# TensorE takes over more of the neighbour sums of a two-layer attention kernel

## The reference, cut to what matters

```python
# layer 0, per dilation: kp, vp are the nine shifted copies of k and v, zero outside the image
attn = softmax(einsum('bhdn,bhdkn->bhnk', qh, kp) * scale)
out = einsum('bhnk,bhdkn->bnhd', attn, vp)        # a sum of nine products per pixel
x = x + concat(outs[i] * gate[:, i])
# layer 1: 4 heads of 32 channels
p = W_qkv @ gn(x) + b_qkv                         # q = k = v = p
att = softmax(p @ p.T / 16)                       # 32x32 per head
x = x + W_proj @ (att @ p) + b_proj
```

## Time and profile before

| | |
|---|---|
| median of three runs | 83.10 us (83.10 to 83.11) |
| the profiled execution | 83.13 us, span 81.3 us |
| VectorE busy | 67.5 us, 83% |
| TensorE busy (matmul) | 71.1 us, 87% |
| GpSimd busy | 41.5 us, 51% |
| ScalarE busy | 29.3 us, 36% |

### The profile page before, as it was taken

The page is one execution under the profiler, slowest core; times in us unless marked ns, Lnnn a source line. Parts: engine busy times, 40 slices in busy tenths (PEclk is TensorE's granted clock), DMA queues, the critical chain, the costliest instruction groups (busy, mean ns, idle before and its releaser), DMA issues.

```text
span 81.3 us, 2474 instructions
## 1 busy us (share of the span) xinstructions
PE 71.1 (87%) x1010; PEld 51.4 (63%) x1010; DVE 67.5 (83%) x184; ACT 29.3 (36%) x92; POOL 41.5 (51%) x84
## 2 busy tenths in 40 slices
PE   4999998799995698999969797879999999999950
PEld 4999753466742466776857664567676868575530
DVE  2152999999999989999999699889999888597850
ACT  1762765963384000000030003230994271764200
POOL 7104018912930037999999999699990005100000
PEclk9999999999999999999999999999999999999999
DMA  1980055000000000000000000000000000012253
GB/s 27 315 286 18 0 120 142 7 0 8 0 0 4 0 12 0 0 0 4 8 0 0 0 0 0 8 0 0 0 0 8 0 0 12 0 57 72 73 194 129
DMA packets 2796, 3.06 MB, mean 38 GB/s; under 512 B 352, under 2 KB 2400, under 8 KB 2784
## 3 DMA queue, kind: packets, MB, share of 16 engines
q1 hardware_dynamic: 2496, 2.63, 10.5%
q10 hardware_dynamic: 288, 0.26, 0.9%
HBM read 1.84 MB, written 1.05 MB: 36 GB/s over the span
## 4 chain that ended last, share of the span: by engine, by line
DVE 54%; PE 28%; POOL 7%; issue 5%; ACT 2%; POOLq 0%
PE ps L815 27%; DVE qk L602 18%; DVE pv L643 12%; POOL rstd L342 3%; POOL acc L379 3%; DVE acc L655 3%; DVE pv L655 2%; DVE x L674 2%; DVE prob L622 2%; DVE smax L609 2%; DVE ssum L619 2%; POOL pv L379 2%; DVE sums L570 1%; DVE acc L643 1%; PE ps L972 1%
## 5 line engine op out<-in xcount | busy, mean ns | idle before, releaser
L815 PE MATMUL ps<-prob,sel 64*128 64x192 f32 (+6 forms) x192 | 17.8, 313 | 2.7 <-DVE pv L643 1.6
L643 DVE TENSOR_TENSOR pv<-ps,v 128x128 f32<-128x128 f32 (+7 forms) x32 | 17.1, 567 | 1.8 <-PE ps L815 0.8
L815 PEld LDWEIGHTS ps<-prob,sel 64*128 64x128 f32 x192 | 13.7, 186 | 6.9 <-DVE pv L643 3.5
L815 PE MATMUL ps<-xn,wp 128*32 128x256 f32 (+1 forms) x208 | 17.1, 384 | 0.9 <-ACT q L417 0.7
L815 PE MATMUL ps<-idle 128*128 128x128 f32 x82 | 14.6, 328 | 1.1 <-DVE idle L533 1.1
L379 POOL TENSOR_TENSOR pv<-pv 128x240 f32<-128x240 f32 (+3 forms) x24 | 14.1, 600 | 0.5 <-DVE pv L643 0.5
L815 PEld LDWEIGHTS ps<-idle 128*128 128x128 f32 x82 | 12.6, 231 | 2.4 <-DVE idle L533 1.1
L342 POOL TENSOR_TENSOR rstd<-gvar,mhalf 128x2 f32<-128x2 f32 (+1 forms) x6 | 4.9, 809 | 15.9 <-DVE gvar L549 15.9
L379 POOL TENSOR_TENSOR acc<-acc,pv 128x256 f32<-128x256 f32 (+4 forms) x20 | 12.7, 640 | 0.5
L815 PEld LDWEIGHTS ps<-xn,wp 128*32 128x32 f32 (+1 forms) x208 | 8.7, 116 | 6.1 <-ACT xn L443 1.3
L602 DVE TENSOR_TENSOR qk<-q,k 128x672 f32<-128x672 f32 (+7 forms) x21 | 11.4, 607 | 0.0
(11 more groups left out here) (82 smaller groups left out, 89.6 us busy)
## 6 DMA issues: line engine op xcount, KB each, us to landing
out_dram<-x SPq DMA_DIRECT2D x8, 128.0 KB, 1.8
gx<-x_dram SPq DMA_DIRECT2D x2, 256.0 KB, 4.4
gx<-x_dram ACTq DMA_DIRECT2D x2, 128.0 KB, 3.1
sel<-selc_dram SPq DMA_DIRECT2D x4, 64.0 KB, 2.2
wp<-wpack_dram SPq DMA_DIRECT2D x1, 194.0 KB, 4.2
gx<-x_dram SPq DMA_DIRECT2D x1, 192.0 KB, 2.8
wp<-wpack_dram SPq DMA_DIRECT2D x1, 131.0 KB, 2.2
gx<-x_dram SPq DMA_DIRECT2D x1, 128.0 KB, 3.0
```

What stands on the lines that cost most here:

```text
L643: last = nc.vector.tensor_tensor(o, a, b, ALU.mult)
L815: return nc.tensor.matmul(o, w, m, start=start, stop=stop)
```

## The change

- GpSimd sums (0,0) to (0,3) and (1,0) whole as before, and does only the first five adds of (1,1) (`POOL_ADDS`). None of the second half's other sums are its work. Its two roots stand after the eighth add of (1,0) and the third of (1,1).
- `add_neighbours` is gone from VectorE. `add_last` makes six adds after the last multiply: column sums of (1,2) and (1,3).
- `restore` and `sum_second` become `add_tiles`: 32x32 tiles everywhere. The first half is brought back in one go, behind `spread(1,1,1)`. In the second half TensorE adds slots 4, 3, 5, 1, 7 of (1,2), 4, 3, 5, 1, 0, 2, 7 of (1,3) and 4, 1, 7, 8 of (1,1); it does so for batches j = 0, 1 first (group 2) and then for j = 2, 3 (group 3), each in an early and a late list.
- The order on all engines: projections of group 0 stand between the last spreads; the rest of groups 0 and 1 stands behind the sums. All `keep_clock` calls after the first half's last spread are gone. One more `norm` is on VectorE.

```diff
-NORMS_ON_DVE = ((2, 0), (3, 0), (3, 1))
-NORMS_ON_ACT = ((0, 0), (0, 1), (1, 0), (1, 1), (2, 1))
+NORMS_ON_DVE = ((2, 0), (2, 1), (3, 0), (3, 1))
+NORMS_ON_ACT = ((0, 0), (0, 1), (1, 0), (1, 1))
...
-POOL_SUMS = (ND, 2)
-
-RSQRT_AFTER = ((1, 0, 4), (1, 1, 0))
+POOL_ADDS = ((8, 8, 8, 8), (8, 5, 0, 0))
+
+RSQRT_AFTER = ((1, 0, 7), (1, 1, 2))
...
@@ ScalarE's order @@
             for i in range(2):
+                copy_projection(0, i)
+            for i in range(2):
                 norm(1, i)
...
             squares(2)
             squares(3)
+            for i in range(2):
+                copy_pT(0, i)
+            for i in range(2):
+                copy_projection(1, i)
+            copy_projection(2, 0)
+            attention_exp(0)
...
@@ VectorE @@
                 if ph and chunk == 0:
-                    dve.wait_ge(added, ADDS * (s + 1))
+                    dve.wait_ge(added, added_by(0, s))
+                    if s == LAST_UNIT:
+                        dve.wait_ge(restored, SLOTS)
...
-            def add_neighbours(ph, s):
...
-            def add_last_column():
...
+            def add_last():
+
+                steps = ((2, 7, 6, 0), (3, 7, 6, 0), (2, 1, 0, 0), (2, 7, 8, 1), (3, 7, 8, 2), (2, 1, 2, 3))
                 dve.wait_ge(pv_ready, 12 * PHASES)
...
-            multiply_pv(1, 1, 0)
+            for i in range(2):
+                multiply_pv(1, 1, i)
             first_residual(0)
-            multiply_pv(1, 1, 1)
-            second_variance(0)
             first_residual(1)
             multiply_pv(1, 1, 2)
+            second_variance(0)
+            multiply_pv(1, 2, 0)
             second_variance(1)
-            for i in range(2):
-                multiply_pv(1, 2, i)
+            multiply_pv(1, 2, 1)
             second_norm_bias(0)
-            second_norm_bias(1)
             multiply_pv(1, 2, 2)
             multiply_pv(1, 3, 0)
-            add_neighbours(1, 2)
+            second_norm_bias(1)
             for i in range(1, 3):
                 multiply_pv(1, 3, i)
-            add_last_column()
+            add_last()
+            first_residual(2)
+            second_variance(2)
+            first_residual(3)
+            second_norm_bias(2)
+            for i in range(2):
+                norm(2, i)
+            second_variance(3)
             attention_shift(0)
+            second_norm_bias(3)
+            for i in range(2):
+                norm(3, i)
+            attention_divide(0)
...
@@ TensorE @@
+            def add_tiles(ph, tiles, js, stop, finished=False):
+
+                for s, slot in tiles:
+                    if slot == 4:
+                        t, first, (r0, r1), (c0, c1) = acc, (ph * ND + s) * N, (0, H), (0, W)
+                    else:
+                        ci, ri = divmod(slot, 3)
+                        t, first, (r0, r1), (c0, c1) = pv[s], slot * N, valid_rows(s, ri), columns(DIL[s], ci)[:2]
                     dims = [[W, r1 - r0], [1, c1 - c0]]
                     at = r0 * W + c0
-                    for j in range(SLOTS):
+                    for j in js:
                         rows = slice(32 * j, 32 * j + 32)
-                        last = mm(view(ps, 512 * (BANK[2] + j) + at, dims, 32 * s, 32), ident[rows, rows],
-                                  view(t, first + at, dims, 32 * j, 32), start=start, stop=stop)
-                        if stop and s == LAST_UNIT:
+                        last = mm(view(ps, 512 * (BANK[GROUPS // PHASES * ph] + j) + at, dims, 32 * s, 32),
+                                  ident[rows, rows], view(t, first + at, dims, 32 * j, 32),
+                                  start=slot == 4, stop=(s, slot) in stop)
+                        if finished and (s, slot) == tiles[-1]:
                             last.then_inc(restored, 1)
...
-            spread(1, 1, 0)
-            restore(0)
-            spread(1, 1, 1)
+            for i in range(2):
+                spread(1, 1, i)
...
+            pe.wait_ge(added, added_by(0, LAST_UNIT))
+            add_tiles(0, [(s, 4) for s in range(ND)], range(SLOTS), stop=[(s, 4) for s in range(ND)], finished=True)
+            spread(1, 1, 2)
             group_stats(0)
-            restore(1)
-            spread(1, 1, 2)
+            spread(1, 2, 0)
             group_stats(1)
...
-            for i in range(2):
-                project_second(0, i)
+            project_second(0, 0)
+            spread(1, 3, 1)
+            project_second(0, 1)
+            spread(1, 3, 2)
+            ends = ((0, 4), (1, 8), (2, 7), (3, 7))
+            early = [(2, 4), (3, 4), (2, 3), (3, 3), (2, 5), (3, 5), (0, 4), (3, 1), (3, 0), (3, 2)]
+            pe.wait_ge(pv_ready, 12 * PHASES - 1)
+            pe.wait_ge(added, added_by(1, 0))
+            add_tiles(1, early, range(2), stop=ends)
+            pe.wait_ge(last_added, 6)
+            pe.wait_ge(added, added_by(1, 1))
+            add_tiles(1, [(2, 1), (1, 4), (3, 7), (1, 1), (2, 7), (1, 7), (1, 8)], range(2), stop=ends, finished=True)
+            add_tiles(1, early, range(2, SLOTS), stop=ends)
+            group_stats(2)
+            add_tiles(1, [(2, 1), (1, 4), (3, 7), (1, 1), (2, 7), (1, 7), (1, 8)], range(2, SLOTS), stop=ends, finished=True)
+            for i in range(2):
+                transpose(0, i)
             for i in range(2):
                 project_second(1, i)
+            group_stats(3)
+            project_second(2, 0)
+            attention(0)
+            project_second(2, 1)
+            transpose(1, 0)
+            project_second(3, 0)
+            transpose(1, 1)
+            project_second(3, 1)
+            for i in range(2):
+                transpose(2, i)
+            attention(1)
             for i in range(2):
                 fuse(0, i)
...
```

More of the change, by code:

```diff
@@ L219, in build @@
         added = sem("added")
-        dve_added = sem("dve_added")
         last_added = sem("last_added")
@@ L940, in tile @@
                             last.then_inc(restored, 1)
-                pe.wait_ge(pv_ready, 12 * PHASES)
-                pe.wait_ge(added, ADDS * sum(POOL_SUMS))
-                pe.wait_ge(dve_added, ADDS)
-                for s in range(ND):
-                    tile(s, acc, (ND + s) * N, start=True, stop=s != LAST_UNIT)
-                s = LAST_UNIT
-                for slot in (3, 5, 1, 0, 2, 7):
-                    ci, ri = divmod(slot, 3)
-                    if slot == 7:
-                        pe.wait_ge(last_added, 2)
-                    tile(s, pv[s], slot * N, *valid_rows(s, ri), *columns(DIL[s], ci)[:2], stop=slot == 7)
@@ L1067, in _ @@
+            add_tiles(1, early, range(2, SLOTS), stop=ends)
+            group_stats(2)
+            add_tiles(1, [(2, 1), (1, 4), (3, 7), (1, 1), (2, 7), (1, 7), (1, 8)], range(2, SLOTS), stop=ends, finished=True)
+            for i in range(2):
+                transpose(0, i)
             for i in range(2):
                 project_second(1, i)
-            for i in range(2):
-                transpose(0, i)
-            for i in range(1, 3):
-                spread(1, 3, i)
-            transpose(1, 0)
@@ L1081, in _ @@
-            keep_clock(2, BANK[1] + 1)
-            group_stats(2)
-            finish(0, 0)
-            keep_clock(2, BANK[1] + 1)
-            group_stats(3)
-            finish(0, 1)
-            keep_clock(1, BANK[1] + 1)
+            for i in range(2):
+                transpose(3, i)
+            attention(2)
+            for i in range(2):
+                finish(0, i)
             for i in range(2):
                 fuse(1, i)
+            attention(3)
             for i in range(2):
-                project_second(2, i)
@@ L1092, in _ @@
-            transpose(2, 0)
-            project_second(3, 0)
-            transpose(2, 1)
-            project_second(3, 1)
-            attention(2)
-            for i in range(2):
-                transpose(3, i)
-            finish(1, 0)
-            attention(3)
-            finish(1, 1)
+                finish(1, i)
             for i in range(2):
```

99 lines of the change are left out of this document (29 added, 70 removed).

## The result

The changed kernel takes 92.69 us in the median (91.92 to 93.07), the kernel before 83.1; the ratio is 1.116, 95% interval 1.107 to 1.125. The direction was as forecast, the size was not: 92.7 lies far outside 82.9 to 86.0. The profiled execution took 91.92 us with a span of 90.0.

A forecast was written before the change was run, and what follows sets the result against it. VectorE (54% of the chain) and TensorE (28%) were taken as the bound; VectorE's gain is eaten by TensorE's queue, so the last residual moves from 79.06 to 80.8, +1.7 us on 83.13: 84.8 us, range 82.9 to 86.0.

The forecast's parts named there:

- a rival with 0.05: TensorE's clock falls to the lower level, doubling 5 to 8 us of its work, partly hidden: 87 to 89 us; chance 0.05.
- TensorE has gaps then, at most 1.0 us by my schedule (50.9 to 51.9, waiting for squares): With fillers gone, TensorE idles at most 1.0 us, which costs nothing unless the clock falls.
- The last product: VectorE's last product ends at 59.2 us instead of 63.17, one small step of six caught beside GpSimd; span 58.8 to 60.1.
- the second root: VectorE waits some 0.3 us at the second bias for GpSimd's second root, ahead of (1,3)'s later chunks.
- Later than forecast, 86: Rival: all small steps are caught beside GpSimd and the spreads wait longer, 86 us; chance 0.10.
- VectorE free 3.2 us sooner: After the last product, `add_last` takes 1.25 us and ends at 60.5 us, where VectorE's adds had ended at 63.69.
- The sums: Second half on TensorE: each list lasts as long as its fullest column group, early 1.3 us, late 1.6 us, both run twice.
- tiles don't run side by side: Rival: the 32x32 tiles' column groups run in turn, early list 2.8 us, late 2.4, total 87 us; chance 0.04.
- What has moved behind: After `project_second(3,0)` starts at 69.75 us, TensorE has 9.8 us of work and 0.7 of waits; last residual ends at 80.8.
- The faster: Rival: layer 0's last residual sets the end and TensorE's backlog fits into its gaps, 82.5 us; chance 0.13.
- the same rival: Rival: lists take 1.2 us instead of 1.6 and VectorE has no new waits, 83.1 us; chance 0.08.
- the gaps without them cost nothing: After the first half's last spread, TensorE's gaps without fillers, at most 1.0 us, cost nothing unless the clock falls.

The follow-up runs named there:

- the run with short additions: Changed kernel, no fillers, 11 of GpSimd's 13 second-half additions cut to two elements: three executions 84.50 to 84.54 us, one 92.09; ratio 1.019.
- the single round: Changed kernel with fillers in all three gaps, second half's sums made once for all four batches instead of twice for two: 84.53 us, ratio 1.019.
- the reordered kernel: Kernel before with (1,2)'s sums moved to TensorE in one round and the engines' lists in a new order: 82.49 us, ratio 0.995.

## Why the prediction was wrong in size, step by step

**The clock.** The fall was a rival with 0.05. Its condition is met: the stage behind 58.4 us runs at half pace. The step that failed is "TensorE has gaps then, at most 1.0 us by my schedule (50.9 to 51.9, waiting for squares)", and with it the 0.05 for a fall. I had listed the gap of 0.92 and missed 0.34 and 1.23 us, since I took VectorE as never idle and did not ask whether TensorE is, while VectorE is at steps that no spread waits for. In the 17.1 us at half pace TensorE was busy 16.7, work of some 8.3 us at full clock, against the 5 to 8 counted. What was mis-sized is the part that others hide: 87 to 89 us let 2.2 to 4.2 of 5 to 8 us reach the end, and 5.95 of some 8.3 did.

The Trainium skill, page TensorE: Matmul & The Clock Gate, section "Part 1: The HAM clock gate", says that the throttle is the resting state and that activity lifts it. The traces agree as far as gaps precede the fall. They differ in what follows it: TensorE was busy for 4.00 of 4.00 us from 68 to 72 and the granted clock stayed at 0.50; by the page alone one would have counted on an early return.

**The last product.** Recorded 59.2, with one small step of six caught beside GpSimd, and 60.1 with all. Measured at full clock 60.25 with fillers in all gaps and 60.09 with them in the second alone. Four of six were caught. In the run with short additions one of six was caught, and the distance of 8.82 us, counted from 50.40 as in the changed kernel, gives 59.2, the recorded value. So the count was the term that failed: two of six in the old order (0.8 us together, not the 0.9 of the recorded sum) said little on the new one. That the rest meets 59.2 is in part luck. VectorE does not wait for the second root at all, where 0.3 us were counted, and the run with short additions has waits of 0.17, 0.40 and 0.73 us ahead of the three chunks of (1,3), where 0.6 was counted for the last alone. The Trainium skill, page SBUF — State Buffer, section "SBUF: two separate sides", had given 60.1 by its rule of mutual exclusion. The trace agrees with it (0.16 us alone, 0.60 beside GpSimd); applied to the new order it was a better guide than the share in the old one. This is 0.9 to 1.05 of the 1.2 us between 84.8 and the 85.97 at full clock. Without the fall it is the rival "Later than forecast, 86" (0.10) that comes closest.

**VectorE free 3.2 us sooner.** 2.2 at full clock (61.51 against 63.69). It is reached only because layer 1 moved behind the sums; where it didn't, VectorE got 0.57.

**The sums.** Confirmed within 0.1 us (1.86 against 1.8 from `add_last` to the first residual): a list lasts as long as its fullest column group. That tiles don't run side by side is refuted.

**What has moved behind.** Confirmed: 11.05 us from `project_second(3,0)` to the end, as forecast. That it is the queue and the two rounds, not VectorE, that set the end, is shown by the single round (1.0 us less behind the common products, and still 3.3 us lost behind group 3's statistics) and by the reordered kernel. The faster and the same rival fall with it.

**Fillers.** That the gaps without them cost nothing holds for the kernel before (ratio 1.000) and not for the changed one.

## What to carry over

When work is taken off one engine, write down the other engine's idle time instant by instant, and not only its busy sum: the adds that were removed had kept TensorE's queue fed and covered it. Small steps between two products of a chain cost more than their time, as they leave gaps on the engine that waits for the product; put them where nobody waits, or beside no GpSimd instruction. If a change drops filler matmuls, look at the granted clock of the new kernel first: one filler line can be worth more than the change.

## What the runs showed of the hardware

- Two gaps of 0.34 and 1.23 us between 54.0 and 56.3 us, with 0.73 us of matmuls between them, were followed by 17 us at half the clock (in all four executions 0.866 to 0.900 in the mean). With either one filled it held in seven of eight executions, and the eighth had a mean of 0.98.
- It is not the same in every execution: with gaps of 0.92 and 0.68 us three held and one fell to 0.887; with the first half's part alone and fillers behind it fell for 7 us in the profiled execution; in the changed kernel with the same first gap and fillers behind it the profiled one held, and another had a mean of 0.961.
- Behind a gap of 0.88 us (another of 0.42 stood 3.3 us ahead of it) the clock fell for 3.4 us in one profiled execution, and in others behind 0.87 us it held.
- Once down it stayed down under load: from 68 to 72 us TensorE was busy 4.00 of 4.00 us at a granted clock of 0.50.
- A VectorE step of two elements with both inputs in SBUF takes 0.16 us alone and 0.45 to 0.60 while GpSimd adds.
